# First attention of a four-layer kernel: the next batch's values formed in the second score group, the last batch's output in the fourth

## What is computed

```python
q, k, q2, k2, v = (proj(Wq), proj(Wk), proj(Wq2), proj(Wk2), proj(Wv))
q = _apply_rotary(q, cos, sin)          # and k, q2, k2 likewise
...
scores = jnp.einsum('bqhd,bkhd->bhqk', q, k)
scores2 = jnp.einsum('bqhd,bkhd->bhqk', q2, k2)
pattern = scores / Dh * (scores2 / Dh)
...
pattern = jnp.where(causal[None, None, :, :], pattern, 0.0)
z = jnp.einsum('bhqk,bkhd->bhqd', pattern, v)
y = z.transpose(0, 2, 1, 3).reshape(Bx, Tx, C)
return y @ Wproj.T
```

## Time and profile before

| | us |
|---|---|
| median of 3 runs (lowest, highest) | 1502.79 (1500.9, 1506.53) |
| the profiled execution | 1502.44 |
| its span, first to last instruction | 1500.7 |
| PE busy, share of the span | 1144.8, 76% |
| DVE busy | 920.2, 61% |
| POOL busy | 731.4, 49% |
| ACT busy | 702.6, 47% |

### The profile page before, as it was taken

How to read it: one execution, slowest core, us unless ns; L and a number is a source line. 1 busy time by engine, 2 the same in 40 slices (tenths; PEclk the granted TensorE clock), 3 DMA queues, 4 the chain that set the end, 5 groups by cost and what they waited for, 6 DMA issues and landing times. The chain is left out here.

```text
span 1500.7 us, 34855 instructions
## 1 busy us (share of the span) xinstructions
PE 1144.8 (76%) x11356; PEld 734.1 (49%) x11356; DVE 920.2 (61%) x2822; ACT 702.6 (47%) x1485; POOL 731.4 (49%) x712
## 2 busy tenths in 40 slices
PE   0799999999999996548888970849996547888880
PEld 0244444444444443216667660739995315666670
DVE  4376676666667665787777206665556787777302
ACT  0466666766666663712232330945554722222330
POOL 0377777777777773014455750025551014545750
PEclk9999999999999997758899995869998758899995
DMA  6000000000000001301111214000001401111218
GB/s 165 7 2 0 0 0 0 0 0 0 0 0 0 0 2 41 105 12 46 47 48 54 81 36 114 0 0 1 0 0 30 116 8 42 55 44 52 76 40 231
DMA packets 67972, 54.53 MB, mean 36 GB/s; under 512 B 12865, under 2 KB 57281, under 8 KB 67905
## 3 DMA queue, kind: packets, MB, share of 16 engines
q1 hardware_dynamic: 51392, 32.70, 8.0%
q0 software_dynamic: 8192, 16.79, 3.8%
q10 hardware_dynamic: 8320, 4.19, 0.9%
HBM read 32.69 MB, written 20.97 MB: 36 GB/s over the span
## 5 line engine op out<-in xcount | busy, mean ns | idle before, releaser
L353 POOL TENSOR_TENSOR patt_aa<-patt_aa,causal_aa 128x512 f32<-128x512 f32 x256 | 319.1, 1273 | 101.1 <-DVE patt_aa L477 101.1
L477 DVE TENSOR_TENSOR patt_aa<-p_second_aa,first_aa 128x512 f32<-128x512 f32 x384 | 247.4, 686 | 163.4 <-ACT first_aa L410 161.7
L1332 POOL DMA_INDIRECT rows_e<-norm_rows,index_e x128 | 123.2, 963 | 331.6 <-DVE index_e L1043 296.8
L410 ACT ACTIVATE first_aa<-p_first_aa 128x512 f32<-128x512 f32 x384 | 208.6, 596 | 146.9 <-PE p_first_aa L568 143.0
L568 PE MATMUL p_first_aa<-q_t_aa,k_t_aa 32*128 32x512 f32 x768 | 217.3, 642 | 30.5 <-ACT first_aa L410 30.5
L568 PE MATMUL p_second_aa<-q_t_aa,k_t_aa 32*128 32x512 f32 x768 | 233.6, 642 | 0.0
L1339 POOL DMA_INDIRECT ffn_rows<-yb_e,index_e x128 | 129.6, 1012 | 63.0 <-issue 40.2
L1244 PE MATMUL p_cnt_e<-reach_e,ones_e 128*128 128x240 bf16 x448 | 85.6, 326 | 80.5 <-DVE reach_e L1089 80.3
L1165 PE MATMUL p_h_e<-rows_t_e,w_e 128*128 128x512 f32 x256 | 142.0, 675 | 0.2
L587 PEld LDWEIGHTS p_z_aa<-patt_aa,v_aa 128*32 128x32 f32 x3072 | 74.9, 109 | 124.0 <-issue 68.3
L1175 PE MATMUL p_y_e<-w_e,hid_e 128*128 128x128 f32 x1024 | 135.2, 275 | 0.0
(11 more groups left out here) (242 smaller groups left out, 2182.8 us busy)
## 6 DMA issues: line engine op xcount, KB each, us to landing
norm_rows<-norm_n SPq DMA_DIRECT2D x32, 256.0 KB, 2.4
w_e<-L_ffn_w SPq DMA_DIRECT2D x32, 256.0 KB
buf_r<-ffn_rows SPq DMA_DIRECT2D x16, 512.0 KB, 6.1
out<-x ACTq DMA_DIRECT2D x8, 512.0 KB, 8.5
rows_e<-norm_rows,index_e POOLq DMA_INDIRECT x128
ffn_rows<-yb_e,index_e POOLq DMA_INDIRECT x128
b_e<-L_ffn_b SPq DMA_DIRECT2D x16, 64.0 KB
lanes<-c_lanes SPq DMA_DIRECT2D x1, 256.0 KB, 2.8
```

The lines of the kernel that those rows point to most:

```text
L353: pool.tensor_tensor(patt[n % LAG][:, b, :, :], patt[n % LAG][:, b, :, :], causal[:, None, :].broadcast_to([P, 4, P]), ALU.mult).then_inc( ...
L410: act.activation(first[n % 2][:, b, :], p_first[b][:], ACT.Identity).then_inc(first_copied, 1)
L477: dve.tensor_tensor(patt[n % LAG][:, b, :, :].rearrange("p h q -> p (h q)"), p_second[(2 * n + b) % ROOMS][:], first[n % 2][:, b, :], ALU. ...
L1332: pool.indirect_dma_start(rows[lpar][:, j, :], None, norm_rows, bass.IndirectOffsetOnAxis(ap=list_of(l, lpar)[:, j:j + 1], axis=0)).then_i ...
```

## The change

On PE, `values(g + 1)` moves from behind z1 to in front of the third score group (n = 2), and `output(g - 1)` from behind that group to behind z1, the place that the values leave. ACT's `copy_v` moves from behind `copy_first(g, 4)` to behind `copy_first(g, 2)`. DVE's `add_x(g - 1)` moves from behind `product(g, 2)` to behind `product(g, 4)`. The waits on `p_misc` follow: `output` now waits for `v_copied` in place of `xt_copied`, `values` no longer waits for `x_added`, and `turn_xn` waits for `x_added` as well.

```diff
@@ ACT turn @@
                     copy_first(g, 2)
                     if more:
+                        copy_v(g + 1, 1 - par)
                         spread_queries(g + 1, 1 - par, (0, 1))
...
                     copy_first(g, 4)
                     if more:
-                        copy_v(g + 1, 1 - par)
                         copy_keys(g + 1, 1 - par)
@@ DVE turn @@
                     product(g, 2)
+                    product(g, 3)
+                    product(g, 4)
                     if later(g):
                         add_x(g - 1)
-                    product(g, 3)
-                    product(g, 4)
                     product(g, 5)
@@ PE turn_xn @@
                     if later(g):
                         pe.wait_ge(v_copied, PER * g)
+                    if not isinstance(g, int) or g > 2:
+                        pe.wait_ge(x_added, g - 2)
@@ PE values @@
                     pe.wait_ge(xt_copied, g + 1)
-                    if not isinstance(g, int) or g > 1:
-                        pe.wait_ge(x_added, g - 1)
@@ PE output @@
-                    pe.wait_ge(xt_copied, min(g + 3, B) if isinstance(g, int) else g + 3)
+                    pe.wait_ge(v_copied, PER * min(g + 3, B) if isinstance(g, int) else PER * g + 3 * PER)
@@ PE turn @@
                         z(g - 1, 1 - par, 5)
+                    if more:
+                        values(g + 1)
                     scores(g, par, 2)
-                    if later(g):
-                        output(g - 1)
                     z(g, par, 0)
...
                     z(g, par, 1)
-                    if more:
-                        values(g + 1)
+                    if later(g):
+                        output(g - 1)
                     scores(g, par, 4)
```

## The result

| | kernel before | changed kernel |
|---|---|---|
| median (lowest to highest) of 6 runs each, us | 1503.8 (1500.9 to 1506.53) | 1514.93 (1511.25 to 1517.85) |
| the profiled execution, us | 1502.44 | 1513.29 |
| its span, us | 1500.7 | 1511.5 |

The ratio is 1.0071 with a 95% interval of 1.0053 to 1.009. The predicted 1513 and the measured 1514.93 lie 1.9 apart.

The account below looks back on a forecast made before the run. The prediction took a 16.36 us batch of steps, each with its own limit on PE or ACT, as the bound. 29 x 0.39 = 11.3, less 0.43 and 0.36, gave +10.5 us: 1513 us, range 1506 to 1516.5.

Parts of the forecast that it names:

- S1 to S2: Step from the second to the third score group's first matmul on PE: ACT's copy loop, 2.37 us, no room, unchanged.
- S5 to S1: Step from the sixth score group to the next batch's second: keeps its 5.47 us.
- The values in front of S2: Values blocks on PE before the third score group: cost nothing, PE idles 0.66 there; 0.46 us a batch without that cover.
- The output away from S2: Output matmuls no longer behind the third score group on PE: the fourth group comes 0.43 us sooner, step 2.97 to 2.54.
- The early copy of the values: ACT's values copy behind its third score copy, before the spreading of the queries: costs nothing, 0.12 us at the other end.
- rival 3: ACT's values copy delays the spreading of the queries: 0.12 of the 0.43 gone, 3.5 us more, 1516.6; 8%.
- The wait for the add: PE's transposes of xn wait for DVE's add, now behind the fifth score group's product: last score group 0.39 us later.
- S4 to S5: Step from the fifth to the sixth score group on PE: 3.97 us instead of 3.15, 3.88 at the other end.
- The old wait for the copy: PE's transposes of xn, before the last score group, waiting for ACT's copy of the values: 0.36 us a batch.
- rival 1: DVE's add is in time and both PE gains stay, 0.79 us a batch: 22.9 us less, 1480, faster; 6%.
- 2, a smaller loss: The gain at the fourth score group about pays for the loss: net 0.1 to 0.25 a batch, 1505 to 1510 us; 24%.
- 4, the clock: PE's clock falls in the loop after the longer idle time: 2.6 us a batch, 75 us in all, over 1575; 2%.

## Why the prediction was right

**What bounds the kernel.** The reading of one batch as a ring of steps held in each kernel: S1 to S2 at 2.37 and S5 to S1 at 5.46 or 5.47 in all but the one that moved a copy behind C5 and the single batch with the lower clock.

**The values in front of S2: nothing.** Right. PE's idle time there took them.

**The output away from S2: 0.43.** Right, 2.97 to 2.54 here, and 0.44 by the experiment that put it back. In its new slot it costs nothing.

**The early copy of the values: nothing, 0.12 at the other end.** Right; rival 3 is out, and the doubled copy shows that it wasn't far off.

**The wait for the add: +0.82 on S4 to S5.** Right to 0.01 in every link (0.63, 1.20, 0.41, 0.16 for 0.15, 0.33 for 0.34). Of the two bounds from the end of the awaited instruction to line 520, 0.06 and 0.15, the row of the same waiting instruction was the one to take: 0.16 measured. The choice was worth 0.09 a batch, 2.6 us. The add started 1.20 behind P4, 0.09 before the end of the product's record, as in the earlier trace rows, and not at its end; a sum that put it at the end would have been 2.6 us too high. The prediction took this for a disagreement with the Trainium skill, "VectorE: DVE Perf Modes", section "The DRAIN you can't avoid", and read it too narrowly: the section goes on to say that a next operation that is not held starts earlier. A start ahead of the record's end doesn't refute it.

**The old wait for the copy: 0.36.** Too small; 0.48. I let the transposes follow the side transposes by 0.58, as scores do. Two experiments show 2.67 from S4 to S5: about 0.1 of the error is there and a few hundredths in S5 behind them (0.31 and not 0.34). It hardly entered the sum, since the new wait swallowed it, but it made rival 1 too small by 29 x 0.12 = 3.5: with the add in time the kernel took 1474, not 1480, of which the rest is within the spread.

**The sum: +10.5.** The measured loop gives 0.39 x 29 = 11.3, as forecast (S1 of the second batch to S1 of the 31st: 474.27 before, 485.56 after). The stage grew by less, 8.6 us. Turn 0 and turn 30 gave back 0.24 and 0.43; in turn 0 the old wait was worth 0.40 (S4 to S5, 3.07 to 2.67), but S2 to S3 grew from 2.45 to 2.61, which the forecast 0.36 left out and no experiment explains. The rest came from the clock and the start: the first scores came 0.77 sooner, PE's clock rose within the first group and not behind it (0.72 from S0 to S1), and z5 of the last batch ran at 0.65 where the earlier trace rows have 1.08. None of this is shown to come from the order, and some runs speak against it: with the changed kernel's order on PE, the kernel with the doubled add took 3.86 from S0 to S1 in the first batch (3.79 before, 3.07 changed) and 1.08 for the last z5. Then 2.2 us came in the stages behind, in which nothing was changed. In the profiled executions of the six kernels run on the first chip that part of the span is between 918 and 925 us, so 2.2 is the spread of single executions. That the profile's difference, 10.8, looks like the forecast 10.5 is in part luck; the medians of six runs, 11.1 apart, say the same with less of it.

**The rivals.** 1, the add in time, was not this kernel but became an experiment. 2, a smaller loss, is out: no link gave way. 4, the clock, is out for this kernel: with 1.11 idle in every batch the granted clock of the stage is 1.00. With 1.44 idle it fell once in 29 batches and cost 1.3 us, so the rival was a real one, but as a single event and not the 2.6 us in every batch by which it was priced.

## What to carry to other kernels

When a step is moved out of a stall, look at who waits for the step that was moved along with it, and what stands behind that waiter in its queue: here an add of 0.41 us, two products late, held up all of PE's queue behind its waiter, and one place earlier in DVE's list turned +0.7% into -1.9%. Count the time from a waiting instruction's own rows, not from a similar one's. A gain and a loss in the same ring add up per turn, so here a table of steps from one turn was enough to forecast the whole.

## What the runs showed of the hardware that I had not expected

PE's clock stayed at the higher level through an idle time of 1.11 in every batch of the changed kernel, and through 28 of the 29 idle times of 1.44 in the kernel with the doubled add; behind the other one it fell, in the middle of the loop. In the tail of the stage z5 followed an idle time of 1.80 or 1.81 in all eight traces. It took 1.08 in three of them (the kernel before, the one with only the values early, the one with the doubled add) and 0.64 or 0.65 in the other five. So in these traces the length of the idle time alone doesn't tell whether the clock falls.

Two chips ran the loop of this stage with the same steps to 0.01 us, but for that one batch, while the kernel before took 1503 on one and 1583 on the other. In the profiled executions the difference lies in the stages behind: 1002 and 1000 us on the second chip against 918 to 925 on the first. Its cause is open.
